# Mixer: C-weighted states summed token-major by accumulating transposes, then turned back onto the skip term

## The reference, cut to what matters

```python
def step(h, t):
    delta_t, B_t, C_t, u_t = t
    dA = jnp.exp(delta_t[:, :, None] * A[None, :, :])
    dBu = delta_t[:, :, None] * B_t[:, None, :] * u_t[:, :, None]
    h = dA * h + dBu
    y = jnp.einsum('bds,bs->bd', h, C_t)
    return (h, y)
...
y = _selective_scan(x, delta, Bm, Cm, A)
y = y + x * D[None, None, :]
y = y * _silu(z)
out = y @ W_out
```

## Time and profile before

| | |
|---|---|
| median of 3 runs | 5237.82 us (5236.78 to 5240.89) |
| span of the profiled execution | 5236.4 us |
| that execution's time beyond its span | not recorded; the median lies 1.4 us above the span |
| PE busy | 5093.7 us (97%) |
| DVE busy | 4729.5 us (90%) |
| ACT busy | 3830.1 us (73%) |
| POOL busy | 4028.2 us (77%) |
| mean granted TensorE clock | 0.994 |
| mixer, scans and sums | from about 711 us to about 4627 us |

### The profile page before, as it was taken

One profiled execution on the slowest core, in us unless ns is written; L12 is line 12 of the kernel. 1 busy time (PEld: TensorE's weight loads), 2 busy tenths in 40 slices (PEclk: granted clock), 3 DMA queues, 4 the chain that ended last, 5 costly groups with the idle time before them and its releaser, 6 DMA issues. The chain is left out here.

```text
span 5236.4 us, 76648 instructions
## 1 busy us (share of the span) xinstructions
PE 5093.7 (97%) x22144; PEld 4077.0 (78%) x22144; DVE 4729.5 (90%) x8180; ACT 3830.1 (73%) x9592; POOL 4028.2 (77%) x1701
## 2 busy tenths in 40 slices
PE   8999989999999999999999999999999999989999
PEld 6777767777777777777777777777777777768887
DVE  6777679999999999999999999999999999977775
ACT  5566468888888888888888888888888888744443
POOL 1111069999999999999999999999999999931110
PEclk9999999999999999999999999999999999989999
DMA  2222231111111111111111111111111111111111
GB/s 83 96 73 83 99 109 45 45 45 53 57 53 49 45 45 45 45 45 45 50 52 48 46 52 55 53 54 45 45 45 45 45 45 45 65 53 57 65 57 41
DMA packets 137370, 291.71 MB, mean 56 GB/s; under 512 B 23280, under 2 KB 40688, under 8 KB 136944
## 3 DMA queue, kind: packets, MB, share of 16 engines
q1 hardware_dynamic: 136944, 286.75, 16.5%
HBM read 218.53 MB, written 68.18 MB: 55 GB/s over the span
## 5 line engine op out<-in xcount | busy, mean ns | idle before, releaser
L948 POOL TENSOR_TENSOR mx_dbu<-mx_bs,mx_du 128x2048 f32<-128x2048 f32 (+1 forms) x513 | 2326.9, 4536 | 60.0 <-DVE mx_hp L1245 49.8
L1154 ACT ACTIVATE mx_ps_da<-mx_dl,mx_a 128x256 f32<-128x256 f32 x4096 | 1775.8, 465 | 53.8 <-DVE mx_hp L1245 19.0
L1245 DVE TENSOR_TENSOR_SCAN mx_hp<-mx_ps_da,mx_hst,mx_dbu 128x256 f32<-128x256 f32 x1792 | 1313.9, 733 | 30.9 <-ACT mx_ps_da L1154 30.9
L1245 DVE TENSOR_TENSOR_SCAN mx_ps_da<-mx_ps_da,mx_hst,mx_dbu 128x256 f32<-128x256 f32 x1792 | 1248.8, 736 | 21.6 <-ACT mx_ps_da L1154 15.7
L961 POOL TENSOR_TENSOR mx_hp<-mx_hp,mx_cs 128x1024 f32<-128x1024 f32 (+1 forms) x576 | 1224.7, 2133 | 1.7 <-ACT mx_hst L1077 1.7
L1395 PE MATMUL mx_ps_y<-mx_hc,mx_ident 128*128 128x256 f32 x4096 | 1054.7, 380 | 2.0 <-ACT mx_ps_y L1016 2.0
L1362 PE MATMUL mx_ps_m<-mx_u,mx_w_dt 128*128 128x256 f32 x4096 | 927.7, 380 | 2.3 <-issue 2.3
L1395 PEld LDWEIGHTS mx_ps_y<-mx_hc,mx_ident 128*128 128x128 f32 x4096 | 779.9, 190 | 109.8 <-ACT mx_ps_y L1016 2.8
L1362 PEld LDWEIGHTS mx_ps_m<-mx_u,mx_w_dt 128*128 128x128 f32 x4096 | 779.2, 190 | 109.4 <-issue 3.1
L1405 PE MATMUL mx_ps_y<-mx_hp,mx_ident 128*128 128x256 f32 x2816 | 787.3, 383 | 50.6 <-POOL mx_hp L961 50.5
L1405 PEld LDWEIGHTS mx_ps_y<-mx_hp,mx_ident 128*128 128x128 f32 x2816 | 525.6, 190 | 233.3 <-issue 87.9
(11 more groups left out here) (122 smaller groups left out, 7378.5 us busy)
## 6 DMA issues: line engine op xcount, KB each, us to landing
mx_bs<-bc_scratch SPq DMA_DIRECT2D x128, 512.0 KB, 4.6
mx_cs<-bc_scratch SPq DMA_DIRECT2D x128, 512.0 KB, 3.8
mx_hT<-hT_scratch SPq DMA_DIRECT2D x32, 518.0 KB, 4.2
hT_scratch<-f_h2T SPq DMA_DIRECT2D x16, 1024.0 KB, 9.1
mx_xo<-xs_scratch SPq DMA_DIRECT2D x32, 512.0 KB, 3.6
x_scratch<-mx_xo SPq DMA_DIRECT2D x32, 512.0 KB, 2.9
f_x<-in_L_attn_inp SPq DMA_DIRECT2D x12, 1024.0 KB, 6.6
...
```

The lines of the kernel that those rows point to most:

```text
L948: G.tensor_tensor(dbu[:, n % NM:n % NM + k].rearrange("p n s t -> p (n s) t"), bs[:, g:g + k].rearrange("p n s t -> p (n s) t"), bcast(du[ ...
L1154: ins = A.activation(ps_da[DA_BANK[p]][:, k, :], dl[:, b % NL, :], ACT.Exp, scale=a_sb[:, b, s:s + 1])
L1245: ins = V.tensor_tensor_scan(da if half == 0 else hp[:, n % NH, k, :], da, dbu[:, n % NM, s, :], 0.0 if first else hst[:, b, SG * g + s:SG ...
```

## The change

All C-weighted states of a unit, four in place of three or four, are now added up by TensorE with transposes that accumulate (`turn_onto`): the product is the stationary operand and the identity moves, once per state and 128 tokens, so that the y bank holds the sum token-major. The first transpose of a block starts the bank anew. Nothing is added on VectorE: `add_state` and `ADDED` are gone. When the sums of a block are complete, ScalarE copies the bank to SBUF (`copy_y` into `mx_yt`), writes the skip term into the bank in channel-major form (`skip`, moved from unit 4b+3 to 4b+9), and TensorE turns the copy back onto it with two more accumulating transposes (`turn_back`). `gated` moves from unit 4b+9 to 4b+10. GpSimd's instructions stay as they are. `ALL_IN_PSUM` is an empty tuple, so the branches on it emit nothing.

```diff
-        SKIP_AT = [NG * b + NG - 1 for b in range(ND)]
-        ADDED = [[n for n in range(NG * b + 1 + (b % 2 == 0), NG * (b + 1))] for b in range(ND)]
-        YG_AT = [NG * b + NG + 5 for b in range(ND)]
+        YT_AT = [NG * b + NG + 5 for b in range(ND)]
+        BACK_AT = [NG * b + NG + 5 for b in range(ND)]
+        YG_AT = [NG * b + NG + 6 for b in range(ND)]
...
+            def copy_y(c, b):
+
+                act.wait_ge(s_r, NU * c + NG * (b + 1))
+                A.activation(yt[:, b % 2, :], y_sum(b), ACT.Copy).then_inc(s_yt, 1)
+
             def skip(c, cp, b):
 
                 act.wait_ge(s_u, ND * c + 2 * (b // 2) + 2)
-                if not (is0(c) and b < 2):
-                    act.wait_ge(s_g, ND * c + (b - 1))
+                act.wait_ge(s_yt, ND * c + (b + 1))
                 A.activation(y_sum(b), u[:, cp, b, :], ACT.Copy, scale=d_sb[:, b:b + 1]).then_inc(s_yd, 1)
...
-                            for bb, s in due(SKIP_AT, n, i):
+                            for bb, s in due(YT_AT, n, i):
+                                copy_y(i + s, bb)
                                 skip(i + s, (par + s) % 2, bb)
...
-            def add_state(c, b, k):
-
-                y = y_sum(b)
-                if k == 0:
-                    dve.wait_ge(s_r, NU * c + NG * (b + 1))
-                else:
-                    dve.wait_ge(s_ya, added_before(c, b) + k)
-                V.tensor_tensor(y, y, hp[:, ADDED[b][k] % NH, SG - SD - 1, :], ALU.add).then_inc(s_ya, 1)
-
             def gated(c, cp, b):
 
                 q = gy[:, cp, b, :]
                 dve.wait_ge(s_zs, ND * c + (b + 1))
-                dve.wait_ge(s_ya, added_before(c, b + 1))
+                dve.wait_ge(s_yb, ND * c + (b + 1))
...
+            def turn_onto(b, pair, first):
+
+                for k in range(SD):
+                    for j in range(TJ):
+                        ins = M.matmul(y_sum(b)[:, j * P:(j + 1) * P], pair[:, k, j * P:(j + 1) * P], ident[:, :],
+                                       is_transpose=True, start=(first and k == 0 and j == 0), stop=False,
+                                       skip_group_check=True)
+                return ins
+
             def sum_psum_states(c, n):
 
                 b, g = divmod(n, NG)
-                if g == 0:
-                    pe.wait_ge(s_yd, ND * c + (b + 1))
+                if g == 0 and not (is0(c) and b < 2):
+                    pe.wait_ge(s_g, ND * c + (b - 1))
                 pe.wait_ge(s_m2, NU * c + (n + 1))
-                for k in range(SD):
-                    ins = M.matmul(y_sum(b), ident[:, :], hc[:, n % NC, k, :],
-                                   start=False, stop=False, skip_group_check=True)
-                ins.then_inc(s_rc, 1)
+                turn_onto(b, hc[:, n % NC], g == 0).then_inc(s_rc, 1)
...
+            def turn_back(c, b):
+
+                pe.wait_ge(s_yd, ND * c + (b + 1))
+                for j in range(TJ):
+                    ins = M.matmul(y_sum(b)[:, j * P:(j + 1) * P], yt[:, b % 2, j * P:(j + 1) * P], ident[:, :],
+                                   is_transpose=True, start=False, stop=(j == TJ - 1), skip_group_check=True)
+                ins.then_inc(s_yb, 1)
```

More of the change, by code:

```diff
@@ L41 @@
 NC = 4
+NX2 = 2
 NH = 8
@@ L759, in mixer_phase @@
         s_m2 = sem("psum_states_times_c")
+        s_m2x = sem("second_psum_states_times_c")
+        s_rcx = sem("second_psum_states_summed")
+        s_kdx = sem("second_psum_state_kept")
         s_pr = sem("sbuf_states_times_c")
@@ L799, in mixer_phase, with in_psum, extra, step_to @@
         DA_BANK = [p % NA for p in range(2 * NU - 1)] + [1]
+        ALL_IN_PSUM = ()
+        NE = len(ALL_IN_PSUM)
+        def in_psum(p):
+            return p % 2 == 0 or p % (2 * NU) // 2 in ALL_IN_PSUM
+        def extra(n):
+            return sum(m < n for m in ALL_IN_PSUM)
+        def step_to(n):
+            k = 1
+            while n - k in ALL_IN_PSUM:
+                k += 1
+            return k
+        def last_in_sbuf(n):
+            while n % NU in ALL_IN_PSUM:
+                n -= 1
+            return n
         def is0(i):
@@ L952, in times_c, with times_c_sbuf @@
             def times_c(c, n):
+                if not in_psum(2 * n + 1):
+                    times_c_sbuf(c, n)
+            def times_c_sbuf(c, n):
                 b, g = divmod(n, NG)
@@ L1193, in epilogue @@
                         keep(LAST, NU + n - KEEP_LAG)
+                    for b in due_after(YT_AT, n):
+                        copy_y(LAST, b)
+                        skip(LAST, LAST % 2, b)
             over_chunks(act, prologue, body, epilogue)
@@ L1258, in times_c, with times_c_second @@
                                 ALU.mult).then_inc(s_m2, 1)
+            def times_c_second(i, n):
+                g, e = n % NG, extra(n)
+                dve.wait_ge(s_sc, 2 * NU * i + (2 * n + 2))
+                if not (is0(i) and e < NX2):
+                    dve.wait_ge(s_rcx, NE * i + (e - NX2 + 1))
+                V.tensor_tensor(hx[:, e % NX2, :, :], ps_da[DA_BANK[2 * n + 1]][:, :, :], cs[:, g, SD:SG, :],
+                                ALU.mult).then_inc(s_m2x, 1)
             def prologue():
@@ L1309, in epilogue @@
                     for b in due_after(YG_AT, n):
-                        for k in range(len(ADDED[b])):
-                            add_state(LAST, b, k)
                         gated(LAST, LAST % 2, b)
@@ L1453, in body @@
                         sum_psum_states(i - 1, NU + n - SUMC_LAG)
+                    for b, s in due(BACK_AT, n, i):
+                        turn_back(i + s, b)
             def epilogue():
-                for n in range(SUM_LAG):
+                for n in range(BACK_AT[-1] + 1 - NU):
+                    if n < SUM_LAG:
+                        sum_states(LAST, NU + n - SUM_LAG)
+                    if n < SUMC_LAG:
+                        sum_psum_states(LAST, NU + n - SUMC_LAG)
+                    for b in due_after(BACK_AT, n):
+                        turn_back(LAST, b)
                     if n == 2:
```

79 lines of the change are left out of this document (39 added, 40 removed).

## The result

The changed kernel takes 5293.3 us (median of four runs, 5292.3 to 5296.4) against 5239.4 us for the kernel before on the same chip: a ratio of 1.0105, 95% interval 1.0091 to 1.0119. It is 1% slower, where 0.7% faster was forecast (5202 us, range up to 5248). The span of the profiled execution is 5292.2 us, the mean granted clock 0.971 (before 0.994).

A forecast was written before the change was run, and what follows sets the result against it. VectorE with a stretch of ScalarE was taken as the limit, GpSimd close behind. Per eight units -0.64 + 0.32 = -0.32 us, times 4 x 28 = 35.8 us off 5236.4, plus 1.4: 5202 us, range 5186 to 5248.

The forecast's parts named there:

- What bounds the kernel: Mixer: VectorE with one stretch of ScalarE sets the pace in 28 chunks, GpSimd 1.4% behind; GpSimd limits the other four.
- VectorE's additions: VectorE's queue: 640 additions removed, 0.32 us each, five per eight units; only those of even blocks gain.
- Odd block 0: Odd blocks: three additions (0.96 us) lie where VectorE would wait for ScalarE's table loads; removing them gains 0.
- Even block 2 x 0.32: Even blocks: no table load, ScalarE is ahead, so two removed additions gain 0.64 us per eight units.
- The gating's 0.32 us in odd blocks: Odd blocks: moved a unit on, the gating leaves the stretch covered by ScalarE and costs VectorE 0.32 us per eight units.
- ScalarE's copy and skip term: ScalarE, unit 4b+9: 0.82 us between the halves of exponentials, covered by its wait for VectorE's product with C; cost 0.
- TensorE's sums: TensorE, per block: 5.8 us of sums become 34 transposes of 0.1 us, 3.4 us; work falls from 15.1 to 12.7.
- The gating, moved one unit on: VectorE, unit 4b+10: no wait for the turn back; the bank's next owner waits when TensorE would stand idle anyway.
- TensorE's clock: Slower rival: gaps lower TensorE's clock; one fall per block fits, two give +256 us, about 5490; chance 0.16, including slow transposes.
- The gap ahead of the gate product: TensorE, after the sums: the gate product waits for the convolution's last step, a gap of over 3 us in every block.
- The rule weighed there: Trainium skill's rule that transposes do not count as PE-busy; it would make clock falls usual on TensorE; given part of 0.16.
- The signs: Right: POOL's scan waits under 0.3 us per eight units. Wrong: clock under 0.9, VectorE idle naming TensorE, gating awaiting turn back.

The follow-up runs named there:

- experiment 12: The changed kernel with only the odd blocks' gatings put back one unit, even ones left, no filler: 5175.6 us, ratio 0.9878.
- experiment 13: The kernel before with VectorE's 256 additions of even blocks left out, so the sum over states is incomplete: 5196.2 us, ratio 0.9919.
- experiment 1: The changed kernel with the fourth out product of a chunk (part 3) one unit later, in NU+8 in place of NU+7: 5199.6 us, ratio 0.9922.
- experiment 7: The changed kernel with 29 unused accumulating transposes ahead of part 3 of the out product, filling its gap: 5238.4 us.
- experiment 8: The changed kernel with all gatings put back one unit, into unit 4b+9, the out products left: 5242.0 us, ratio 1.0007.
- experiment 11: The changed kernel with all gatings put back and 4 unused matmuls ahead of the gate product in even blocks' units alone: 5193.1 us, ratio 0.9911.
- experiments 6: The changed kernel with 12 unused accumulating transposes ahead of part 3 of the out product, leaving a 2.0 us gap: 5244.4 us.
- experiment 3: The kernel before, sums still on VectorE, with part 3 of the out product one unit earlier: 5237.6 us, ratio 0.9997.

## Why the prediction was wrong, point by point

**What bounds the kernel: right.** VectorE with ScalarE's table loads set the pace, and GpSimd was the next limit by a hair; experiment 12 reached it. With the old sums TensorE was as near: in experiment 13 it is busy 130.34 of 130.91 us.

**VectorE's additions: right.** Odd block 0: measured 2.4 us of 5238.7, within the noise. Even block 2 x 0.32: in the trace without these additions two of a chunk's four stretches of eight units take 29.91 us (2305.48 - 2275.57) against 30.57, 0.66 less. The other two take 30.31 and 30.74 us (before 30.84 and 30.57), so that a chunk takes 120.87 us in place of 122.55, and 42 us were measured where 4 x 28 x 0.66 would be 74. By then GpSimd is busy 130.23 of 130.91 us, TensorE 130.34, and ScalarE waits for the input product 186.5 us in all against 42.6; which of them keeps the rest wasn't separated. The gating's 0.32 us in odd blocks: putting it back (experiment 12 against 1) is worth 24 us of 35.8, with GpSimd as the new limit. Together, once the wait is out of the way, 5199.6 us and a chunk of 121.24 us against the forecast 5202 and 121.3.

**ScalarE's copy and skip term: right.** They lie in its wait for VectorE's product, which is 631.6 us in all before and 439.3 in experiment 1; the copy itself has to wait only once.

**TensorE's sums: right.** Accumulating transposes take 0.44 us per four, 0.109 each (29 of them in experiment 7 give the third digit), close to the 0.1 assumed:

```profile
2400.79 0.60 PE L1425 MATMUL mx_ps_y<-mx_ident,mx_hp 128*128 128x128 f32 x4
2401.23 0.60 PE L1425 MATMUL mx_ps_y<-mx_ident,mx_hc 128*128 128x128 f32 x4
```

**The gating, moved one unit on: this is the step that failed.** The prediction asked what the gating itself waits for ("no wait", which was right for this place) and named the bank's next owner as the one that waits for it, at no cost. It left out its second reader. Each block's gating also feeds the out product, and for the last block that product stood two units behind the gating and now stands one unit behind, at the head of TensorE's unit. The out product has no term in the sum at all. The missing term is 94 us (5293.3 against 5199.6 us): 24 to 29 us for the wait, 1.03 us in an ordinary chunk, by what is queued behind the product (input product, first tap, exponentials, scans), and the rest for the clock that falls in it.

**TensorE's clock: right in kind, wrong in place and price.** The rival had one fall per block swallowed by spare time (14.5 of 15.3 us) and decided only at two. That compares sums of work, and no sum was exceeded: PE is busy 113.89 of 130.91 us in the changed kernel. A fall costs when someone waits for the very products that run in it. There, one per chunk, not per block, costs 1.69 or 2.89 us of chunk time, 51.5 us over 23 ordinary chunks. The gap ahead of the gate product exists, but it was predicted at over 3 us in every block and is 1.6 us on the mean (322 us in 200 waits, up to 2.7 us each; 23.8 us in 52 waits before). It cost nothing that shows in experiment 1, since the turn back and the gating behind it still have a unit to spare; with that unit gone (experiment 8) the same gap costs 49 us (experiment 11 against 8). The gap that decided was another.

**The rule weighed there** falls too. The trace and experiments 6 and 7 show a granted clock of 1.00 through 3.3 us of nothing but transposes. The Trainium skill, "TensorE: Matmul & The Clock Gate", Part 4: PE-mode transpose, has it that the full clock does not engage for them; no run here agrees. What lowered the clock was that TensorE stood still.

**The signs.** POOL's wait for scans was to fall and rose from 49.8 to 119.4 us; that one did tell. Of those named for "wrong", the profile showed none as worded: the clock of the ordinary stretch above is 0.99, no VectorE idle in the steady mixer names TensorE (it names ScalarE, one link on), and the gating waits for the turn back twice in all, 7.9 us. A chain of three engines shows at its end only the last link; ScalarE's waits, 179.5 us naming L1366, were the row to look at, and no sign had been set for ScalarE's first tap.

**Open.** Why the falls last 3.4 us in one chunk and 6.8 in the next, in turn, isn't settled, nor what tells the 9 of 22 equal gaps that lower the clock from the other 13. Neither part of the change was run alone in its place: the later gating with the old sums is an estimate from rows (experiment 3), and a changed kernel with slower sums wasn't tried.

## What to carry to other kernels

When an instruction is moved later, list every reader of its result, with the place at which each asks for it and what is queued behind it; here one of the eight parts of the out product was left one unit behind its gating, and that cost 94 us where the rest of the change gained 38. Compare the reader's place on its own engine with the end of the moved step's unit on the other: the rows of the kernel before give the wait, 3.0 us by them and 3.27 measured. Making an engine faster that nobody waits for isn't neutral either: ahead of the gate product TensorE's gaps grew from 23.8 to 322 us in all, and where a step had no time to spare behind such a gap (experiment 8), the lower clock cost 49 us. Once that shows, the remedy is an order in which the waiting product stands behind the ones that others need, or one in which the moved step goes back where it is free.
